# A recurrence stage reordered: half products in two parts, the sum of the output between the masked products, x loaded one step sooner

## The reference

```
q, k, v = x @ Wq, x @ Wk, x @ Wv            # 16 heads of 16
fg = sigmoid(x @ Wf + bf)
def step(state, (qt, kt, vt, gt)):
    state = state * gt[..., None] + vt[..., None] * kt[..., None, :]
    return state, einsum('bhij,bhj->bhi', state, qt)
out = layernorm(scan(step, zeros)) * gamma + beta
out = (out * silu(x @ Wg)) @ Wout
x = layernorm(x + out)
x = layernorm(x + cross_attention(x, ctx))
x = layernorm(x + feed_forward(x))           # with weights and activations rounded to a grid
```

## Time and profile before

| | us |
|---|---|
| median of 3 runs (2257.58 to 2268.09) | 2265.29 |
| the profiled execution, its own time | 2278.17 |
| its span, first to last instruction | 2276.5 |
| PE busy | 2128.0 (93%) |
| DVE busy | 1585.4 (70%) |
| ACT busy | 1203.2 (53%) |
| POOL busy | 324.3 (14%) |

### The profile page before, as it was taken

The page is one execution under the profiler, slowest core; times in us unless marked ns, Lnnn a source line. Parts: engine busy times, 40 slices in busy tenths (PEclk is TensorE's granted clock), DMA queues, the critical chain, the costliest instruction groups (busy, mean ns, idle before and its releaser), DMA issues. The chain is left out here.

```text
span 2276.5 us, 74145 instructions
## 1 busy us (share of the span) xinstructions
PE 2128.0 (93%) x30007; PEld 1428.7 (63%) x30007; DVE 1585.4 (70%) x2916; ACT 1203.2 (53%) x1951; POOL 324.3 (14%) x312
## 2 busy tenths in 40 slices
PE   7999999989999869999999999999899999999798
PEld 4666666666666657777777777776444444444587
DVE  6766666676766746677676777766555557998887
ACT  4443444444443336666667666675221218888565
POOL 1321100110100111111111111111000004410021
PEclk9988899899998879999999999999899999999999
DMA  3100000010010010100101011010000004469674
GB/s 108 31 21 22 26 26 22 21 31 22 26 26 21 21 47 30 42 28 28 41 28 41 28 34 35 28 41 1 1 0 0 0 0 165 195 238 424 246 269 160
DMA packets 78311, 146.48 MB, mean 64 GB/s; under 512 B 10035, under 2 KB 63542, under 8 KB 78134
## 3 DMA queue, kind: packets, MB, share of 16 engines
q1 hardware_dynamic: 78134, 143.70, 18.0%
HBM read 82.84 MB, written 60.82 MB: 63 GB/s over the span
## 5 line engine op out<-in xcount | busy, mean ns | idle before, releaser
L1310 PE MATMUL ff_bank<-ff_xq,w_uh 128*128 (+1 forms) x1536 | 456.9, 379 | 1.0 <-ACT ff_whole L1419 1.0
L1310 PE MATMUL ff_bank<-ff_xq,w_ul 128*128 (+1 forms) x768 | 291.1, 379 | 0.0
L1310 PEld LDWEIGHTS ff_bank<-ff_xq,w_uh 128*128 128x128 f16 x1536 | 149.7, 98 | 178.9 <-issue 1.4
L1629 DVE TENSOR_REDUCE ff_top<-ff_bank 128x512 f32 (+1 forms) x192 | 132.6, 691 | 115.8 <-PE ff_bank L1310 115.7
L600 DVE TENSOR_TENSOR x<-rec_x,rec_until 128x512 f32<-128x512 f32 x256 | 158.6, 681 | 42.6 <-PE rec_x L348 42.6
L501 ACT ACTIVATE x<-rec_e,rec_hidden 128x512 f32<-128x512 f32 x256 | 155.7, 700 | 37.9 <-PE rec_e L364 37.7
L1091 DVE TENSOR_REDUCE mneg<-att_s 128x4 f32<-128x512 f32 x256 | 158.9, 683 | 20.6 <-PE att_s L848 19.8
L636 DVE TENSOR_TENSOR rec_tmp<-rec_x,x 32x256 f32<-32x256 f32 (+1 forms) x192 | 80.8, 421 | 131.0 <-PE rec_x L402 65.0
L325 PE MATMUL rec_f<-w_rec,rec_xT 128*128 128x512 f32 x256 | 165.1, 781 | 6.0 <-DVEq L540 4.7
L376 PE MATMUL rec_x<-x 32*32 32x64 f32 x8192 | 146.4, 218 | 12.8 <-DVE x L600 8.6
L376 PEld LDWEIGHTS rec_x<-x 32*32 32x32 f32 x8192 | 124.8, 107 | 47.8 <-issue 47.6
(11 more groups left out here) (236 smaller groups left out, 4385.7 us busy)
## 6 DMA issues: line engine op xcount, KB each, us to landing
gate_scratch<-ff_out SPq DMA_DIRECT2D x28, 768.0 KB, 3.4
ff_in<-gate_scratch SPq DMA_DIRECT2D x28, 768.0 KB, 11.2
product_scratch<-ff_out SPq DMA_DIRECT2D x28, 768.0 KB, 10.8
ff_out<-product_scratch SPq DMA_DIRECT2D x28, 768.0 KB, 6.0
att_x<-in_x SPq DMA_DIRECT2D x32, 256.0 KB, 2.7
att_ctx<-in_ctx SPq DMA_DIRECT2D x32, 256.0 KB, 2.9
att_o<-rec_scratch SPq DMA_DIRECT2D x32, 256.0 KB, 3.7
out<-s_out SPq DMA_DIRECT2D x16, 512.0 KB, 3.3
```

Source lines behind the costliest of these rows:

```text
L1310: m = T.matmul(bank_[:], weights(wp, kc, a, c), tile[:, xp, kc], start=(i == 0), stop=(i == len(terms) - 1))
L1629: V.tensor_reduce(top[:, k, bass.ds(n, 1)], banks[k % 6][:], AX.X, ALU.max, apply_absolute_value=True).then_inc(q1["maxed"], 1)
```

## The change

The recurrence's arithmetic stays the same. PE's `across_half` is cut in two by heads, one part ahead of `value_gate(p + 1, 0)` and one behind it, and the two parts of `across_quarter` are put between `exponents` 3, 4 and `value_gate(p + 1, 1)`. On DVE `total(n - 1)` moves from the end of a step to the next step, between `scores_out(n, 0)` and `scores_out(n, 1)`; `floor(p, 0)` moves to the end of the step before; `half_out` moves behind `weighted(p, s, 0)`. On SP the load of a pair is issued ahead of the store that it stood behind, so that it runs three pairs ahead of the pair stored. In the attention, DVE's `residual(n0, ...)` moves ahead of `apply`.

```diff
-                with sp.Fori(0, NP // 2 - 1) as j:
+                sp.wait_ge(q["x_made"], 1)
+                load(2, 0)
+                with sp.Fori(0, NP // 2 - 2) as j:
                     for u in range(2):
-                        sp.wait_ge(q["x_made"], 2 * j + u + 1)
-                        load(2 * j + 2 + u, u)
+                        sp.wait_ge(q["x_made"], 2 * j + u + 2)
+                        load(2 * j + 3 + u, 1 - u)
                         store(2 * j + u, u)
-                store(NP - 2, 0)
-                store(NP - 1, 1)
+                sp.wait_ge(q["x_made"], NP - 2)
+                load(NP - 1, 1)
+                for p in range(NP - 4, NP):
+                    store(p, p % 2)
...
-                def across_half(n):
-                    pe.wait_ge(q["w_ready"], 2 + 2 * n + 2)
-                    pe.wait_ge(q["o_taken"], TAKES * n + TAKES + 1)
-                    pe.sem_inc(q["seen"], 1)
+                def across_half(n, part):
+                    if part == 0:
+                        pe.wait_ge(q["w_ready"], 2 + 2 * n + 2)
+                        pe.wait_ge(q["o_taken"], TAKES * n + TAKES + 1)
+                        pe.sem_inc(q["seen"], 1)
                     halves = (slice(0, 2 * CH), slice(2 * CH, P))
-                    for hd in range(H):
+                    for hd in range(part * HH, (part + 1) * HH):
...
-                    m.then_inc(q["o_made"], 1)
+                    if part == 1:
+                        m.then_inc(q["o_made"], 1)
...
                     if back:
-                        across_half(n)
-                        across_quarter(n, 0)
+                        across_half(n, 0)
                     if more:
                         value_gate(p + 1, 0)
                     if back:
+                        across_half(n, 1)
+                    if front:
+                        exponents(p, s, 3)
+                    if back:
+                        across_quarter(n, 0)
+                    if front:
+                        exponents(p, s, 4)
+                    if back:
                         across_quarter(n, 1)
-                    if front:
-                        exponents(p, s, 3)
-                        exponents(p, s, 4)
                     if more:
                         value_gate(p + 1, 1)
...
                     if front:
-                        floor(p, 0)
+                        if not back:
+                            floor(p, 0)
                         floor(p, 1)
                     if back:
                         scores_out(n, 0)
+                        if not isinstance(p, int) or p > 1:
+                            total(n - 1)
                         scores_out(n, 1)
...
-                        half_out(n, so)
...
                     if front:
                         weighted(p, s, 0)
                     if back:
+                        half_out(n, so)
                         quarter_out(n, so)
+                    if front and not (isinstance(p, int) and p == NP - 1):
+                        floor(p + 1, 0)
+                    if back and not front:
                         total(n)
...
                         stats(res1, st_1, mv_1, q["var_1"], q["c_stats_1"], p)
+                    if attn:
+                        residual(n0, so, 0, p - 1)
+                    if front:
                         wait_if(dve, q["x1b_ready"], p)
                         apply(res1, mv_1, rs_1, q["rstd_1"], x1, q["x1_ready"], p)
                     if attn:
-                        residual(n0, so, 0, p - 1)
                         stats2(n0, 0)
                         apply2(n0, 0)
```

More of the change, by code:

```diff
@@ L442, in pieces @@
                     if back:
-                        across_quarter(n, 1)
+                        across_half(n, 1)
                     if front:
                         exponents(p, s, 3)
+                    if back:
+                        across_quarter(n, 0)
+                    if front:
                         exponents(p, s, 4)
+                    if back:
+                        across_quarter(n, 1)
                     if more:
@@ L675, in step @@
                     if back:
+                        half_out(n, so)
                         quarter_out(n, so)
+                    if front and not (isinstance(p, int) and p == NP - 1):
+                        floor(p + 1, 0)
+                    if back and not front:
                         total(n)
-                steps(dve, step)
+                step(0, 0, 0, True, False)
+                step(1, 1, 0, True, True)
+                step(2, 0, 1, True, True)
+                with dve.Fori(0, (NP - 4) // 2) as j:
+                    for u in range(2):
+                        step(2 * j + 3 + u, (1 + u) % 2, j + 1 + u, True, True)
+                step(NP - 1, 1, (NP - 2) // 2, True, True)
+                step(NP, 0, NP // 2, False, True)
 def attention_block(nc, t, x_d, ctx_d, o_d):
```

## The result

| | before | changed |
|---|---|---|
| median, fast runs | 2266.69 us | 2227.85 us (2225.19 to 2230.62, 4 runs) |
| ratio | | 0.9836, 95% interval 0.9804 to 0.9867 |
| profiled execution | 2278.17 us | 2225.19 us |
| mean granted clock in it | 0.958 | 0.976 |

The kernel became 1.6% faster, 39 us where 52 were forecast; the range held it. Between them lie 40.0 us in the 29 steps of the recurrence, 2.7 at the two ends of its pipeline, 9.8 in the attention from its first to its last residual (737.5 and 727.7 us) and 0.5 in the rest.

What follows compares the result with a forecast made beforehand. PE was taken to set the pace, slowed by waits and a clock at 1.2 GHz; -46 (clock) -3 (step, x) +5 (POOL clash) -8 (attention) = -52 us off the median 2265.29 gave 2213 us, range 2195 to 2257.

Steps and rivals of the forecast that it cites:

- clock: PE in the recurrence: shorter runs of tiny matmuls win back four fifths of 57 us lost at 1.2 GHz, 46 us.
- clean step and x waits: Recurrence: full-clock step from 21.93 to 21.88 us, and waits for x gone; 3 us saved in all.
- clash with POOL: Recurrence: POOL's gather and levelling now hold DVE's split and weighting; +5 us once, bounds 0 and 12.
- attention: Attention: the earlier residual lets PE's values start 0.27 us sooner a step; 8 us saved, bounds 0 and 18.
- carried over to the median: Whole kernel: the 52 us reckoned for the profiled execution were taken equally off the median, 2265.29, giving 2213 us.
- rival A: PE in the recurrence: clock falls as often, tiny matmuls only stand elsewhere; 2259 us, chance 0.13.
- The masked products and `total`: DVE in the recurrence: first masked products at T+1.16, scores(n, 1) at T+3.69, inside(0) at T+6.05; 0.19 us saved.
- the tight end of the step: Recurrence: the next step's scores wait for the last quarter product; +0.14 us a step, bounds 0 and 0.5.
- The load of x: SP in the recurrence: loading one step sooner removes the waits for x, 8.8 us at best.
- rival D: SP in the recurrence: the sooner load, mostly hidden, does nothing by itself; 3 us, inside the forecast, no own chance.
- Rival B: PE in the recurrence: work between the value_gates drops the clock too, two falls a step; 2301 us, chance 0.07.
- C: Whole kernel: full clock recovery, the residual worth its whole wait, no POOL clash; -78 us, 2187 us, chance 0.06.

Runs made afterwards that it cites:

- levelling_late: The changed kernel, but in the first eight steps POOL's operation on the weight matrix waits for DVE's weighting that it blocked; 2209.98 us, ratio to before 0.976.
- attention_undone: The changed kernel with the residual behind apply again in the attention; 2227.5 us, ratio to before 0.9832.
- half_behind: exponents_behind with value_gate 0 first and all half and quarter products behind it in one piece; 2261.83 us, ratio to before 0.9986.
- pe_order_undone: The changed kernel with PE's order of before; DVE, SP and attention stay changed; 2253.78 us.
- load_behind_store: The changed kernel with SP's order of before, a pair's load behind the store of the pair three back; 2408.6 us, ratio to before 1.0616.
- half_ahead: exponents_behind with both half parts ahead of value_gate 0 again and both quarter parts behind it; 2199.76 us, ratio to before 0.9715.
- exponents_behind: levelling_late with half part 1 and both quarter parts in one piece, exponents 3 and 4 behind them, ahead of value_gate 1; 2197.77 us, ratio to before 0.9708.

## Why the prediction was right, and where not

By its own steps, for the two profiled executions, in us:

| step | forecast | measured | by |
|---|---|---|---|
| clock | -46 | -50, without the clash's share | PE at half 114 before, 13 in `levelling_late` |
| clean step and x waits | -3 | -2 and a few | 21.93 to 21.85; no wait for x is left |
| clash with POOL | +5 | +13 to +17, with its falls | `levelling_late`; two steps of 30.2 instead of 21.85; +8 in the profile of `attention_undone` |
| attention | -8 | -7.7 | `attention_undone` |
| the ends of the pipeline | 0 | -3 | last two steps 809.70 - 767.34 = 42.4 us before, 767.01 - 729.83 = 37.2 after; but the first addition comes 2.5 us later, at 59.74 instead of 57.22 |
| carried over to the median | 0 | about +11 | the clocks of 56 executions of before |

The lines for the profiled pair add up to about 50 of the 53 us; the attention as a whole lost 9.8 us between the two profiles, 2 more than its edit accounts for. All are read from single executions, so a few us of them are noise.

*The clock* was the right mechanism, and the fall was read rightly as coming from thin work, not from idling; rival A is out: the falls did not move elsewhere, they went. What made the forecast hesitate, the long thin stretch between the `value_gate`s, did no harm: outside the clash, where PE did idle before the fall, the clock fell about once in ten steps. A long thin piece without any wide matmul does harm (`half_behind`).

*The masked products and `total`* came out to 0.01 us: T+1.16, 3.70 and 6.06. That the clean step came out at 21.85 us, 0.03 from the forecast, is partly luck: the changes between wide and thin matmuls cost 0.4 us (21.85 against 21.44 in `pe_order_undone`), not 0.2; against that the tight end of the step cost 0.05 us, not 0.14, and the step of the earlier trace rows held a wait for x of 0.31 us at PE's weight loads, where 0.2 was counted. The price of a change was right, 0.1 us; the count was wrong, since the new order has four more of them and not two.

*The clash* is the failed size: put at 5 us, it cost 13.5 by the medians, just beyond its bound of 12. The hold of the weighting was foreseen, 2.8 us of it reaching PE; 2.4 did. What I left out is that the clock fell behind that wait at both places in all three profiles of this recurrence, and stayed low for 3.4 to 13.7 us. A stall in a place of thin work has to be priced with the clock that it costs.

*The carry to the median* failed: I took 52 us off a median that held less of the loss than the profiled execution. Between clocks 0.958 and 0.963 lie 0.005 x 2 x 2262 = 23 us at half, 11 us of time. With that and the clash as measured, the same sum would have given about 2234 us; 2227.85 was measured.

*The load of x* was priced as hidden, at most 8.8 us, and rival D says that it does nothing by itself. Against the kernel before that holds: no wait for x is left, and there was little to gain. `load_behind_store` shows what I should have asked for each moved wait: who is queued behind it. Moving `total` moves the gather, the store, and on SP the load behind the store. With `total` where it now is, the sooner load is worth 185 us; without it the change would lose.

Rival B needed two falls a step, and there was about one in ten steps; C was refused by the clash and by ACT's exponential.

## What to carry to other kernels

A PE that is busy throughout can still lose its clock to a run of thin matmuls; look at the granted clock beside the timeline and put a wide matmul, already there, into the middle of the run: against PE's order of before, moving a 0.7 us piece (`half_ahead`, beside the other parts of the change) did for the clock what PE's whole reordering did. Before an operation is moved, follow everything that waits for it through the other queues, the DMA queue included, and look for an operation of POOL that will now fall on a DVE instruction with two inputs in SBUF. And a gain in clock is to be taken off a typical execution, not off the profiled one, unless their clocks agree.

## What the runs showed of the hardware beyond that

- A POOL operation (5.4 us by itself, 5.82 there) stretched a DVE instruction of 1.2 us with both inputs in SBUF to 6.38 us; started behind it, each took its own time (1.21 and 5.37 us), and DVE instructions that read PSUM beside it took their usual 0.68 us.
- A change between wide and thin matmuls costs PE about 0.1 us: the clean step is 21.85 us in the changed order and 21.40 in `exponents_behind`, with the same matmuls and four changes fewer.
- A fall of the clock behind the same wait lasted 3.4 us in one execution and 13.6 us in another of the same instructions; the step took 25.9 and 30.2 us.
- Executions of one program spread with their clock: 32 us between clocks 0.954 and 0.969, more than several of the effects sought here.
